# Causal attention with its transfers further ahead: load 8 (was 6), relative product 6 (was 5), skewed read 4 (was 3), and SyncE issuing load, read, write

## The chip, the cores and the metric

The kernel runs on one core of a Trainium2 chip. The metric is device time in microseconds for one execution of the whole program: a two-layer block of attention and feed-forward parts. The change lies in one of its stages, the causal attention of the first layer.

## The reference

```python
# layer 0 attention; q from layernorm(x), k and v from ctx; B=4, S=512, 16 heads of 16, so 64 heads
QEr = jnp.einsum('bhsd,ld->bhsl', q, Er_s)
Srel = _skew(QEr)                          # row i is shifted so that column j holds q_i . Er[511 - (i - j)]
QK = jnp.einsum('bhsd,bhtd->bhst', q, k)
attn = (QK + Srel) / math.sqrt(dh)
attn = jnp.where(causal[None, None], attn, -jnp.inf)
attn = jax.nn.softmax(attn, axis=-1)
out = jnp.einsum('bhst,bhtd->bhsd', attn, v)
# then x = x + out, a top-2-of-8 expert feed-forward, a masked attention and a ternary-weight feed-forward
```

## The kernel before

**The stage.** `causal_attention` takes 64 heads (4 batches of 16), one a step, as a software pipeline. A head is 512 queries by 512 keys, of which only the causal part is made: `CAUSAL_UNITS` packs the row blocks 512, 384+128 and 256 columns wide into three units, 1280 columns (REL_W) on 128 partitions. Queries and keys are held as bf16 pieces in DRAM (`packed`), 96 partitions a head.

**One head's way through the stages:**
1. *Load* (SyncE, line 424, by `load_head`, line 309): the head's queries and keys from DRAM into `qk`, 192 KB; 8 buffers (ROUND).
2. *Relative product* (TensorE `relative`, line 442; ScalarE copy, line 552): Q times Er into `psE`, copied into `stage`, 2 buffers.
3. *Write* (SyncE, line 429): `stage` into the DRAM tensor `rel`, 640 KB; 4 slots (RING).
4. *Skewed read* (SyncE, line 419): `rel` back into `bias`, each partition starting one column earlier, which is the reference's `_skew`; 640 KB; 4 buffers.
5. *Scores* (TensorE, lines 450 and 453, into `psS`) and on VectorE, line 512, scores plus bias with the row maximum.
6. *Exponential* (ScalarE, line 557), one step later.
7. *Transposes* (TensorE, line 464, `psT`; VectorE copy, line 520), another step later, and the weighing of the values by groups of four heads (lines 353, 366, 373, 375).

**What sets the order.** Each engine runs its own `step(n)`, n from -LOAD on. In step n an engine works on head n + k for each stage, k being that stage's lead: LOAD, REL, READ, SOFT (the scores), EXP. `stage_of` gives head, slot and turn. The first and last steps are unrolled, the middle ones loop eight at a time (`run_heads`). Engines keep pace by semaphores alone. On SyncE, which issues all three transfers of a head through one queue and waits in program order, these are:
- the read waits until the head's write has landed, and until VectorE is done with the bias buffer that it overwrites (4 heads back);
- the load waits until TensorE has made the scores of the head 8 back;
- the write waits for ScalarE's three copies, and for the read 4 heads back.

ScalarE waits in front of a head's copies until the write two heads back has landed (line 545), because `stage` has two buffers; its exponentials of the same step stand behind that wait. In the last steps SyncE also fills `slots_in` with zeros for the next stage (line 432).

Of the kernel before, what the change touches and what calls it, by code (L numbers as in the profile page):

```python
# [33 lines left out]
ROUND = 2 * GROUP  # L34
# [10 lines left out]
def wait(eng, sem, value):  # L45

    if isinstance(value, int) and value <= 0:
        return
    eng.wait_ge(sem, value)  # L49


def build(nc, a, out):
# [14 lines left out]
    with top:  # L67
        def sem(name):
            return nc.alloc_semaphore(name)

        def sb(ctx, name, shape, dt=F32):
            return ctx.enter_context(nc.sbuf_tensor(name, shape, dt))
# [211 lines left out]
        def run_heads(eng, first, last, step):  # L284

            for n in range(first, ROUND):
                step(n, n % ROUND, n // ROUND)
            rounds = NBH // ROUND - 2
            with eng.Fori(1, rounds + 1) as it:
                for r in range(ROUND):  # L290
                    step(it * ROUND + r, r, it)
            for n in range((rounds + 1) * ROUND, last + 1):
                step(n, n % ROUND, n // ROUND)

        def stage_of(n, r, it, ahead):

            if isinstance(n, int) and not 0 <= n + ahead < NBH:
                return None
            return n + ahead, (r + ahead) % RING, it * (ROUND // RING) + (r + ahead) // RING
# [8 lines left out]
        def load_head(sp, m, dst, s_qk):  # L308
            sp.dma_start(dst, bass.AP(packed.ap().tensor, m * (DH * 2 * S),
                                      [[B * D * 2 * S, PIECES], [2 * S, DH], [1, 2 * S]])).then_inc(s_qk, 16)  # L310
# [69 lines left out]
        def causal_attention(ErP, identb, dmask):  # L380

            units = CAUSAL_UNITS
            NU = len(units)
# [1 line left out]
            place = {i: (512 * u + off, w) for u, unit in enumerate(units) for i, off, w in unit}  # L385
            key_place = {j: (512 * u + off, w) for u, unit in enumerate(CAUSAL_KEYS) for j, off, w in unit}
            last = NBH + 2 * GROUP
            LOAD, REL, READ, SOFT, EXP = 6, 5, 3, 2, 1
            with ExitStack() as ctx:
                qk = [sb(ctx, f"qk{r}", [KP, 2 * S], BF16) for r in range(ROUND)]  # L390
                stage = [sb(ctx, f"stage{r}", [P, REL_W]) for r in range(2)]
# [9 lines left out]
                s_qk = [sem(f"s_qk{r}") for r in range(ROUND)]  # L401
# [3 lines left out]
                s_emm, s_eev, s_smm, s_soft, s_nm, s_exp, s_tmm, s_tev, s_seen, s_seen_sp = (  # L405
                    sem(f"s_{n}") for n in names)
                block = ctx.enter_context(nc.Block())

                @block.sync
                def _(sp):  # L410
                    def step(n, r, it):
                        if h := stage_of(n, r, it, READ):
                            m, slot, turn = h
                            sp.wait_ge(s_wr[slot], 16 * (turn + 1))
                            sp.sem_inc(s_seen_sp, 1)
                            wait(sp, s_soft, NU * (m - RING + 1))

                            skewed = bass.AP(rel[slot].ap().tensor, P - 1, [[REL_W - 1, P], [1, REL_W]])
                            sp.dma_start(bias[slot][:, :], skewed).then_inc(s_rd[slot], 16)
                        if h := stage_of(n, r, it, LOAD):  # L420
                            m, slot, turn = h
                            wait(sp, s_smm, NU * (m - ROUND + 1))
                            slot = (r + LOAD) % ROUND
                            load_head(sp, m, qk[slot][:, :], s_qk[slot])
                        if h := stage_of(n, r, it, REL):
                            m, slot, turn = h
                            sp.wait_ge(s_eev, NU * (m + 1))
                            wait(sp, s_rd[slot], 16 * turn)
                            sp.dma_start(rel[slot][:, :], stage[slot % 2][:, :]).then_inc(s_wr[slot], 16)
                        if isinstance(n, int) and n + READ == NBH:  # L430

                            sp.dma_start(slots_in[:, :].rearrange("(n p) d -> p n d", p=P),
                                         zero_row[:, :].unsqueeze(1).broadcast_to([P, SLOT_TILES, D])).then_inc(s_zeroed, 16)
                    run_heads(sp, -LOAD, last, step)
# [284 lines left out]
        with ExitStack() as ctx:  # L719
# [108 lines left out]
            with ExitStack() as c0:  # L828
                ErP = sb(c0, "ErP", [KP, S], BF16)
                with nc.cleanup_on_exit():  # L830
                    opening(ErP)
                    causal_attention(ErP, identb, dmask)
# [861 lines left out]
```

## Time and profile before

| what | us |
|---|---|
| median of 3 runs (1341.21 to 1344.07) | 1343.36 |
| the profiled execution, from first to last instruction (its only time on record) | 1343.2 |
| the causal attention stage, by its first load and the next stage's first transfer | 81.07 to 455.07 |
| writes of heads 8 to 63 issued, the steady part | 128.76 to 431.01 |

Over the span PE is busy 1048.0 us (78%), VectorE 696.9 (52%), ScalarE 655.3 (49%). The page cuts the span into 40 slices of 33.6 us; the stage is the third to the fourteenth. Each digit is a share in tenths, and GB/s is what the DMA engines moved:

```profile
PEclk9866978798889777799999999566899999998799
DMA  7477877787778866666656652235311111110001
GB/s 246 163 254 273 287 269 277 255 283 272 264 267 291 320 261 217 218 192 199 211 186 205 206 190 95 79 105 190 100 47 47 47 47 47 44 44 9 0 25 40
```

### The profile page before, as it was taken

The numbers are of one execution on the slowest core, as the hardware profiler recorded it, in microseconds if no ns is written. First come the engines' busy times: TensorE is split into PE (matmuls) and PEld (weight loads), VectorE is DVE, ScalarE is ACT, GpSimd is POOL, SyncE is SP. The second block draws the span as 40 slices with busy tenths as digits, with TensorE's granted clock in tenths as the row PEclk, the third lists the DMA queues.
The fourth block names the chain that finished last, engine by engine and source line by source line (L and its number), as shares of the span: only waits on it lengthen the run. The fifth ranks groups of instructions, "written<-read, shape, count | busy, mean of one in ns | idle before, by whom it ended". The sixth has DMA issues, their size and how long they took to land. (4 is left out here: it accounts for less than half of the span.)

```text
span 1343.2 us, 22770 instructions
## 1 busy us (share of the span) xinstructions
PE 1048.0 (78%) x6434; PEld 648.0 (48%) x6435; DVE 696.9 (52%) x2140; ACT 655.3 (49%) x1346; POOL 224.2 (17%) x531
## 2 busy tenths in 40 slices
PE   6736787777778384699999999133899999997487
PEld 3414444444444252599999998011233333333444
DVE  4825666676667763110111100346766666674687
ACT  2425666666566221233333232132677777763687
POOL 0000000000000026011111111530222222231222
PEclk9866978798889777799999999566899999998799
DMA  7477877787778866666656652235311111110001
GB/s 246 163 254 273 287 269 277 255 283 272 264 267 291 320 261 217 218 192 199 211 186 205 206 190 95 79 105 190 100 47 47 47 47 47 44 44 9 0 25 40
DMA packets 93319, 227.41 MB, mean 169 GB/s; under 512 B 9686, under 2 KB 51766, under 8 KB 87254
## 3 DMA queue, kind: packets, MB, share of 16 engines
q1 hardware_dynamic: 86454, 208.20, 45.1%
q0 software_dynamic: 6816, 18.62, 5.0%
q8 instruction: 22, 0.36, 0.1%
q14 instruction: 27, 0.22, 0.0%
HBM read 143.07 MB, written 83.62 MB: 169 GB/s over the span
## 5 line engine op out<-in xcount | busy, mean ns | idle before, releaser
L684 DVE CUSTOM_DVE_ANT_0 unused<-mpsS,mask_bias 128x512 bf16<-128x512 f32 x256 | 172.1, 691 | 84.0 <-PE mpsS L617 83.8
L711 ACT ACTIVATE mPT<-mpsB 128x512 f32<-128x512 f32 x256 | 152.8, 598 | 81.0 <-PE mpsB L624 74.8
L1358 ACT ACTIVATE hT<-ph,w 128x128 f32<-128x128 f32 x312 | 89.3, 369 | 197.0 <-PE ph L1332 197.0
L512 DVE CUSTOM_DVE_ANT_0 scores<-psS,bias 128x512 f32<-128x512 f32 (+3 forms) x256 | 120.1, 488 | 113.2 <-PE psS L453 57.5
L552 ACT COPY stage<-psE 128x512 f32<-128x512 f32 (+1 forms) x192 | 98.2, 513 | 148.8 <-PE psE L442 144.9
L464 PE MATMUL psT<-ident,scores 128*128 128x128 f32 x640 | 120.9, 310 | 44.5 <-ACT scores L557 42.6
L1332 PE MATMUL ph<-xT,w 128*128 128x128 f32 x1248 | 147.0, 276 | 0.0
L1377 DVE TENSOR_TENSOR ys<-py,b 128x256 f32<-128x256 f32 x39 | 16.6, 425 | 249.3 <-PE py L1342 249.3
L1332 PEld LDWEIGHTS ph<-xT,w 128*128 128x128 f32 x1248 | 143.9, 193 | 0.1
L1342 PE MATMUL py<-w,hT 128*128 x624 | 141.2, 379 | 0.7 <-DVE ys L1377 0.7
L557 ACT ACTIVATE scores<-scores,nm 128x128 f32<-128x128 f32 (+3 forms) x256 | 136.4, 562 | 4.4 <-DVE nm L525 4.4
L442 PE MATMUL psE<-ErP,qk 96*128 96x512 bf16 (+3 forms) x256 | 79.7, 358 | 59.4 <-DMA qk<-packed 58.4
L1342 PEld LDWEIGHTS py<-w,hT 128*128 128x128 f32 x624 | 115.6, 190 | 15.2 <-issue 1.1
L520 DVE COPY PT<-psT 128x512 f32<-128x512 f32 (+1 forms) x192 | 114.7, 599 | 10.7 <-PE psT L464 10.5
L617 PE MATMUL mpsS<-mqk 96*128 96x512 bf16 x256 | 100.7, 395 | 21.2 <-DMA mqk<-packed 15.5
L464 PEld LDWEIGHTS psT<-ident,scores 128*128 128x128 f32 x640 | 77.5, 159 | 69.0 <-ACT scores L557 50.7
L622 PE MATMUL mpsB<-mqk 99*128 99x512 bf16 x256 | 98.8, 386 | 0.1
L624 PE MATMUL mpsB<-maskT,identb 128*128 128x512 bf16 x256 | 98.1, 383 | 0.0
L339 POOL TENSOR_TENSOR spreada<-V,zerosa 128x272 f32<-128x272 f32 x16 | 11.5, 721 | 423.2 <-PE psOa L353 341.5
L450 PE MATMUL psS<-qk 96*128 96x512 bf16 (+3 forms) x256 | 80.8, 341 | 1.0 <-DVE mx L512 0.8
L353 PE MATMUL psOm<-mPT,spreadm 128*32 128x512 f32 x512 | 67.8, 604 | 0.8 <-ACT headsm L360 0.8
L617 PEld LDWEIGHTS mpsS<-mqk 96*128 96x128 bf16 x256 | 25.0, 98 | 87.0 <-DVE mmx L684 36.3
(247 smaller groups left out, 1501.0 us busy)
## 6 DMA issues: line engine op xcount, KB each, us to landing
rel<-stage SPq DMA_DIRECT2D x64, 640.0 KB, 3.8
bias<-rel SPq DMA_DIRECT2D x64, 640.0 KB, 5.6
w<-in_w1p SPq DMA_DIRECT2D x39, 1028.0 KB
qk<-packed SPq DMA_DIRECT2D x64, 192.0 KB
mqk<-packed SPq DMA_DIRECT2D x64, 192.0 KB
w<-in_w2p SPq DMA_DIRECT2D x8, 1024.0 KB
slots_in<-zero_row SPq DMA_DIRECT2D x1, 4992.0 KB, 18.2
xs<-slots_in SPq DMA_DIRECT2D x39, 128.0 KB
```

The costliest lines, as they stand in the source:

```text
L464: tr = nc.tensor.transpose(psT[bank][:, to:to + P], scores[slot][:, at:at + P], ident[:, :])
L512: ttr = nc.vector.tensor_tensor_reduce(out=scores[slot][:, at:at + w], in0=psS[(NU * slot + u) % 2][:, off:off + w], in1=bias[slot][:, at: ...
L520: nc.vector.tensor_copy(PT[r][:, 512 * u:512 * u + WU[u]], psT[(NU * slot + u) % 2][:, 0:WU[u]]).then_inc(s_tev, 1)
L552: nc.scalar.copy(stage[slot % 2][:, 512 * i:512 * i + WU[i]], psE[(NU * slot + i) % 2][:, 0:WU[i]]).then_inc(s_eev, 1)
L557: ex = nc.scalar.activation(scores[slot][:, at:at + w], scores[slot][:, at:at + w], ACT.Exp, bias=nm[:, slot, i:i + 1], scale=1.0 / 4)
L617: nc.tensor.matmul(psS[i % 2][:, :], qk[slot][0:KP, i * P:(i + 1) * P], qk[slot][0:KP, S:2 * S], start=True, stop=True).then_inc(s_smm, 1)
L622: nc.tensor.matmul(psB[i % 2][:, :], qk[slot][:, S + i * P:S + (i + 1) * P], qk[slot][:, 0:S], start=True, stop=False)
L624: nc.tensor.matmul(psB[i % 2][:, :], identb[:, :], maskT[:, i, :], start=False, stop=True).then_inc(s_bmm, 1)
L684: nc.vector.tensor_tensor_reduce(out=unused[:, i, :], in0=psS[i % 2][:, :], in1=mask_bias[:, i, :], scale=1.0, scalar=-3.0e38, op0=ALU.add ...
L711: nc.scalar.activation(PT[r][:, j, :], psB[j % 2][:, :], ACT.Exp, scale=1.0 / 4).then_inc(s_exp, 1)
L1332: mm = nc.tensor.matmul(ph[half][:, q * P:(q + 1) * P], w1[i][:, dk * F + f * P:dk * F + (f + 1) * P], xT[i][:, dk, :], start=(dk == 0), s ...
L1342: mm = nc.tensor.matmul(py[:, 0:D], hT[i][:, f, :], w2[:, bass.ds(e, 1), f * D:(f + 1) * D].rearrange("p a d -> p (a d)"), start=(f == 0), ...
```

## The change

The leads change, so that the load of a head goes out in step m-8 (was m-6), its relative product and write in step m-6 (was m-5), its read in step m-4 (was m-3). Scores, exponentials and transposes keep their steps. SyncE issues load, read, write in each step, where it issued read, load, write. The pipeline starts at step -8. No buffer, size or other instruction changes.

```diff
-            LOAD, REL, READ, SOFT, EXP = 6, 5, 3, 2, 1
+            LOAD, REL, READ, SOFT, EXP = 8, 6, 4, 2, 1
@@
                     def step(n, r, it):
+                        if h := stage_of(n, r, it, LOAD):
+                            m, slot, turn = h
+                            wait(sp, s_smm, NU * (m - ROUND + 1))
+                            slot = (r + LOAD) % ROUND
+                            load_head(sp, m, qk[slot][:, :], s_qk[slot])
                         if h := stage_of(n, r, it, READ):
                             m, slot, turn = h
                             sp.wait_ge(s_wr[slot], 16 * (turn + 1))
@@
                             sp.dma_start(bias[slot][:, :], skewed).then_inc(s_rd[slot], 16)
-                        if h := stage_of(n, r, it, LOAD):
-                            m, slot, turn = h
-                            wait(sp, s_smm, NU * (m - ROUND + 1))
-                            slot = (r + LOAD) % ROUND
-                            load_head(sp, m, qk[slot][:, :], s_qk[slot])
                         if h := stage_of(n, r, it, REL):
```

## Rows read from the trace of the kernel before

**Rows 1.** Window of the steady part: bounds, length, busy by engine, PEclk, DMA share, GB/s

```profile
125.00:431.00 306.00, 234.41 (x1724) 136.87 (x1724) 205.42 (x697) 189.14 (x404) 9.38 (x13) 0.89 0.78 275
```

**Rows 2.** Waits, 125 to 431 us: engine, tile, line, what for, total, times, longest

```profile
ACT stage L552 <- PE psE L442: 113.0, 74, 4.6
PE psE L442 <- DMA qk<-packed: 35.8, 37, 3.2
DVE scores L512 <- DMA bias<-rel: 28.0, 26, 3.3
```

**Rows 3.** Timeline of SyncE's queue (start, length); writes of heads 8, 31 to 34, 63

```profile
128.76 0.33 SPq L429 DMA_DIRECT2D rel<-stage  x1
...
248.54 0.32 SPq L419 DMA_DIRECT2D bias<-rel  x1
249.07 0.85 SPq L309 DMA_DIRECT2D qk<-packed  x1
252.43 0.33 SPq L429 DMA_DIRECT2D rel<-stage  x1
...
261.38 0.33 SPq L429 DMA_DIRECT2D rel<-stage  x1
...
267.39 0.33 SPq L429 DMA_DIRECT2D rel<-stage  x1
...
271.74 0.33 SPq L429 DMA_DIRECT2D rel<-stage  x1
...
431.01 0.32 SPq L429 DMA_DIRECT2D rel<-stage  x1
```

**Rows 4.** Timelines of PE and DVE; in brackets idle time before and its releaser

```profile
202.12 0.39 PE L442 MATMUL psE<-ErP,qk 96*128 96x512 bf16 x1 [0.90 <-DMA qk<-packed]
...
256.05 0.69 DVE L512 CUSTOM_DVE_ANT_0 scores<-psS,bias 128x512 f32<-128x512 f32 x1 [3.26 <-DMA bias<-rel]
...
257.46 0.61 PE L442 MATMUL psE<-ErP,qk 96*128 96x512 bf16 x1 [3.22 <-DMA qk<-packed]
```

**Rows 5.** From issue to landing, 125 to 431 us: the write's line, then the read's

```profile
DMA to landing us min/median/max: 3.1/3.8/6.1
...
DMA to landing us min/median/max: 4.4/5.9/7.7
```

**Rows 6.** Windows of 2 us, columns as in rows 1

```profile
125.00:127.00 2.00, 1.61 (x13) 1.19 (x14) 1.38 (x4) 0.45 (x1) 0.00 (x0) 1.00 1.14 303
...
203.00:205.00 2.00, 2.00 (x12) 1.57 (x11) 1.49 (x6) 1.01 (x4) 0.00 (x0) 0.50 0.61 231
...
255.00:257.00 2.00, 0.00 (x0) 0.00 (x0) 0.95 (x3) 0.00 (x0) 0.00 (x0) 1.00 1.00 351
...
259.00:261.00 2.00, 2.00 (x14) 1.30 (x16) 1.79 (x8) 0.98 (x3) 0.00 (x0) 0.50 0.08 26
...
427.00:429.00 2.00, 1.34 (x11) 0.92 (x12) 1.38 (x4) 0.19 (x1) 0.00 (x0) 1.00 1.03 342
```

**Rows 7.** DMA issues of the page: count, KB each, median us to landing

```profile
rel<-stage SPq DMA_DIRECT2D x64, 640.0 KB, 3.8
bias<-rel SPq DMA_DIRECT2D x64, 640.0 KB, 5.6
...
qk<-packed SPq DMA_DIRECT2D x64, 192.0 KB
```

**Rows 8.** Timelines of PE and DVE at the stage's start and end

```profile
93.55 1.04 PE L442 MATMUL psE<-ErP,qk 96*128 96x512 bf16 x3 [4.31 <-DMA qk<-packed]
...
436.68 0.69 DVE L512 CUSTOM_DVE_ANT_0 scores<-psS,bias 128x512 f32<-128x512 f32 x1 [0.88 <-issue]
...
440.15 0.69 DVE L512 CUSTOM_DVE_ANT_0 scores<-psS,bias 128x512 f32<-128x512 f32 x1
```

**Rows 9.** The step 267.39 to 271.74: ScalarE's first copy, and the step's window

```profile
269.45 0.59 ACT L552 COPY stage<-psE 128x512 f32<-128x512 f32 x1 [0.96 <-PE psE L442]
...
267.39:271.74 4.35, 4.31 (x39) 2.18 (x32) 3.04 (x11) 3.27 (x8) 0.00 (x0) 1.00 0.86 291
```

## The prediction

> **What bounds the kernel now.** I took the stage's place from the page's slices, then read its window, the waits, the issue times of SyncE's queue, and last the two-microsecond windows. The change touches one stage, the causal attention, which lies at 80 to 455 us. In its steady part, 125 to 431 us, no engine is full: PE is busy 234 of 306 us, DVE 205, ACT 189, the DMA share is 0.78 and the granted clock averages 0.89 [rows 1]. So the stage is not limited by one resource's capacity, and what it waits for decides.
>
> The waits name two transfers. PE waits 35.8 us for `qk` (the head's load) in front of the relative product, DVE 28.0 us for `bias` (the skewed read) in front of the first score reduction. ACT's larger wait, 113.0 us for psE, is what they look like one engine further on [rows 2].
>
> One stall in detail shows how. Head 31's write goes out at 252.43 and head 32's only at 261.38, 8.95 us later [rows 3]. Between them DVE stands 3.26 us until head 29's read lands at 256.05, and PE, behind DVE's bank release and its own load, 3.22 us until head 32's load lands at 257.46 [rows 4]. That read was issued at 248.54 and that load at 249.07 [rows 3], so they took 7.5 and 8.4 us; in the steady part a read takes 4.4 to 7.7 us from issue to landing, median 5.9, a write 3.1 to 6.1, median 3.8 [rows 5]. By the code a read is issued one step ahead of its use (READ 3, SOFT 2) and so is a load (LOAD 6, REL 5). One step is 4.35 us when nothing is late (267.39 to 271.74) [rows 3]. A transfer of 5.9 us ordered one 4.35 us step ahead is late; that is the bound: latency under load, at too short a distance.
>
> The stall is paid twice. During it PE is idle (0.00 busy in 255 to 257) and the granted clock then falls from 1.00 to 0.50, 1.2 GHz [rows 6]. At that clock the next step, 261.38 to 267.39, takes 6.01 us although it waits for no transfer [rows 3]. And with the engines late nothing new is ordered: the DMA share falls to 0.08 at 259 to 261 [rows 6], after having been at 1.00. The DMA engines are thus alternately full and empty.
>
> **The pace now.** Head 8's write is issued at 128.76 and head 63's at 431.01: 55 intervals in 302.25 us, 5.50 us a head [rows 3].
>
> **What the change does, part by part.**
>
> *Load 8 ahead, product 6 ahead.* A load now has two steps instead of one before its product. Two steps of 4.35 us are 8.7 us, above even the 8.4 us of the bad case. The buffer: head n+8 takes the slot of head n, whose scores PE makes in step n-2, since SOFT is 2. SP enters step n after ACT's copies of step n-1, so this wait (it had four steps of slack, now two) ends before it is reached. Gain: PE's 35.8 us of waits. New wait: none.
>
> *Read 4 ahead.* A read also has two steps instead of one, 8.7 us against at most 7.7. Its own condition, the write of the same head, stays two steps earlier (6-4 as 5-3), and the bias buffer it overwrites, head n's, was used by DVE in step n-2. Gain: DVE's 28.0 us. It overlaps PE's waits: in the stall above, 3.26 and 3.22 us together cover only 4.7 us, 0.72 of their sum [rows 4], so I count the two as 0.72 x 64 = 46 us.
>
> *Order load, read, write.* The read may stand behind a write that hasn't landed (longest 6.1 us) [rows 5], and then no longer holds up the load. Each issue still costs SP 0.33 us for a write, as much for a read and about 0.8 for a load [rows 3]: about 1.5 us of a step, and SP idles for most of the rest. The read now goes out some 0.9 us later, behind the load's issue. That is covered by the whole step that it gained. If that cover were gone it would be 0.9 us a step, 50 us over the stage; it would need reads over 7.8 us.
>
> *The clock.* A mean of 0.89 between levels 1.00 and 0.50 is 22% of the 306 us, 67 us, at half clock. Steps there take 6.01 instead of 4.35 us: 67 x (1 - 4.35/6.01) = 18 us lost. Without long stalls most of it returns.
>
> *What is late next.* Taking all of both away gives 302 - 46 - 18 = 238 us, 4.33 us a head: the fast step again. But the DMA engines must move 640 + 640 + 192 KB a head, 1.507 MB [rows 7]. Of the 153 windows of 2 us from 125 to 431 us, 54 have a DMA share of 0.95 or more and move on average 326 GB/s; the first, the last and one in the stall stand in [rows 6]. So a full DMA side needs 1.507 / 0.326 = 4.62 us a head. From the mean (275 GB/s at share 0.78) it would be 1.507 / 0.353 = 4.27 us [rows 1]. The slower figure is the nearer one, being measured when full. DMA therefore becomes the bound, with the engines at 4.35 close behind; two near-equal bounds with jitter give somewhat more than either. Bounds for the new pace: 4.35 us (fast step) from below; from above 5.50, no gain. I take 4.8, close to the full-DMA row, plus 0.2 for jitter and an occasional low-clock step.
>
> *Steady part:* 55 x (5.50 - 4.8) = 38 us less.
>
> *Ends.* The pipeline gets one step more between product and scores. At the start head 0 still has to go load, product, write, read, score; what changes is that head 2's load no longer waits for the first write (PE idles 4.31 us for it until 93.55 [rows 8]), so head 8's write comes one step earlier relative to the scores, 5 to 6 us. At the end there is one step more after the last write; steps there have no product and take 3.5 us (436.68 to 440.15 [rows 8]). Net about 2 us less, bounds 0 and 5. The zero fill of slots_in still follows the last read and has the tail's time to itself as now.
>
> Sum: 38 + 2 = 40 us off the profiled span of 1343.2 us, which stands 0.2 us from the median of 1343.36: 1303 us.
>
> **A rule against the rows.** The windows show 326 GB/s with all 16 DMA engines occupied, writes, skewed reads and loads mixed [rows 6]. The Trainium skill (DMA: Bandwidth & Descriptors, section Anatomy of one DMA) gives a variable cost of bytes over 436 GB/s. By it a head needs 3.46 us and DMA would bound nothing. The rows at full share move a quarter less, so the trace disagrees and the sum goes by them.
>
> **Rivals.**
>
> *A. The engines bound, DMA keeps up.* Pace 4.45 (4.35 to 4.5, the shortest steps): 55 x 1.05 + 2 = 60 us less, 1283. For: the mean-share figure of 4.27 us, and transfers that are spread evenly may run better than in bursts. Against: 54 full windows at 326 GB/s. The skill's rate above would lead here.
>
> *B. The clock keeps falling.* At a DMA-bound pace PE still pauses in every step. If it spends the same 22% of time at half clock, the rate is 0.22/6.01 + 0.78/4.8, a pace of 5.02: 55 x 0.48 + 2 = 28 us less, 1315; with 40% low, 5.22: 17 us less, 1326. For: not every fall follows a long stall; 203 to 205 reads 0.50 and the wait ahead of it was 0.90 us [rows 4, 6]. Against: at 267 to 272 PE is busy 4.31 of 4.35 us and keeps 1.00 [rows 9]. The Trainium skill (TensorE: Matmul & The Clock Gate, section A second HAM failure mode: psum-queue depth-cycling) tells of a kernel whose short pauses between groups alone made the clock oscillate; this stage does rotate through two banks per product.
>
> *C. The transfers only get slower.* More of them in flight lengthen each other, as 7.5 and 8.4 us in the stall showed, and the waits return at two steps' distance: pace 5.4 to 5.5, 1337 to 1343. Against: the share of 0.78 and the empty windows.
>
> *D. The write's landing takes over, slower.* ACT may copy head n+6 only when head n+4's write has landed (two stage buffers), and it waits in front of its exponentials, so PE's transposes and DVE's copies stand behind. The loop: first copy to the write's issue takes 2.29 us (269.45 to 271.74 [rows 3, 9]), then the landing L, and two heads pass per turn: pace (L + 2.29)/2. With L 3.8 it is 3.0, with 6.1 4.2: hidden. It decides from L = 2 x 4.8 - 2.29 = 7.3 us, and is slower than before from L = 8.7. Loads and reads ordered earlier stand in front of the write, so L may grow; at 9.2 us the pace is 5.75, 14 us more, 1357. Against: a write would have to take 2.6 us longer than the longest now, and the loop throttles itself before.
>
> *E. The change doesn't do what it says*, for instance a read or load held back by the buffer conditions above. Then pace and time stay; held to be part of C.
>
> **Numbers.** Forecast (pace 4.6 to 5.0) 0.54; A 0.12; B 0.23; C with E 0.06; D 0.05. A measurement of this kernel can tell a change of 0.2%, 2.7 us, from none. Faster: forecast, A, B and a part of C, 0.91. Same: most of C, 0.05. Slower: 0.04. The range reaches from near A, pace 4.5 (1343 - 57 = 1286), to B's bad end with a little over, 1330, leaving out about 0.2.
>
> **What would show it.** PE's waits for qk and DVE's for bias in the stage near zero after the first heads; the pace of SP's write issues near 4.8 with no interval of 7 us; DMA share over 0.9 and 310 GB/s or more; granted clock over 0.95; reads landing later than now (6 us or more) without anyone waiting. Wrong would be: a share of 0.8 with a clock of 1.00 (then the engines bound, A), a clock still at 0.9 or below (B), ACT waiting for the rel DMA at the copy of line 552 (D).

## The result and the profile after

The changed kernel takes 1283.9 us (median of 4 runs, 1282.46 to 1286.1) against 1343.58 us (now of 4 runs): ratio 0.9563, 95% interval 0.9543 to 0.9583. It is faster by 60 us where I had forecast 40, and lies 2 us below the low end of my range. The profiled execution has a span of 1284.6 us.

The slices of the page, now of 32.1 us each; the stage is the third to the thirteenth:

```profile
PEclk9865999999996877999999997576999999998799
DMA  7478889999998657665666641345211111110001
GB/s 247 149 258 307 321 329 337 344 341 339 337 324 329 237 180 240 189 214 185 208 196 195 208 147 50 103 157 155 63 47 46 47 44 48 44 38 9 1 29 39
```

From the fifth slice to the twelfth the clock digit is 9 throughout, where it went up and down, and the DMA engines move 321 to 344 GB/s, where the kernel before moved 255 to 291.

The steady part, between the writes of heads 8 and 63, answers to [rows 1, 3]; these are SyncE's timeline (start, length), and the window between, with its busy times, clock, DMA share and GB/s:

```profile
125.86 0.33 SPq L429 DMA_DIRECT2D rel<-stage  x1
...
371.10 0.32 SPq L429 DMA_DIRECT2D rel<-stage  x1
...
397.23 0.38 SPq L1074 DMA_DIRECT2D mask<-in_mask  x1
```

```profile
125.86:371.10 245.24, 194.69 (x1690) 120.09 (x1691) 201.45 (x684) 180.00 (x399) 9.35 (x13) 1.00 0.91 335
```

55 intervals in 245.24 us are 4.46 us a head, against 5.50. The longest is 5.31 us, where it was 8.95. VectorE's work is the same as before (202 us) in 57 us less. Head 8's write comes 2.9 us earlier, the part from the last write to the next stage's first transfer is 2.1 us longer (26.1 against 24.1, the additional step), and the rest of the program 0.8 us shorter: 57.0 + 2.9 - 2.1 + 0.8 = 58.6 us, the difference of the spans.

The waits of the changed kernel over 200 to 360 us, a part of what [rows 2] cover:

```profile
ACT stage L552 <- DMA rel<-stage: 41.6, 36, 1.3
...
PE psT L464 <- ACT scores L557: 31.4, 36, 1.4
DVE scores L512 <- DMA bias<-rel: 13.6, 23, 0.7
```

PE's wait for `qk` is gone. DVE still waits for `bias`, here never over 0.7 us. What is new stands on top: ScalarE waits in every step of this stretch, 1.16 us on average, for its write two heads back to land (over the whole steady part 60.4 us in 51 waits, the longest 1.7, and DVE 24.2 us in 34, the longest 1.3). PE's transposes wait for ScalarE's exponentials behind it. This is the loop of rival D. It can be read in one step (SyncE's timeline, then ScalarE's):

```profile
246.88 0.32 SPq L429 DMA_DIRECT2D rel<-stage  x1
247.42 0.78 SPq L309 DMA_DIRECT2D qk<-packed  x1
...
253.67 0.33 SPq L424 DMA_DIRECT2D bias<-rel  x1
255.75 0.32 SPq L429 DMA_DIRECT2D rel<-stage  x1
```

```profile
253.69 0.58 ACT L552 COPY stage<-psE 128x512 f32<-128x512 f32 x1 [1.28 <-DMA rel<-stage]
```

The write issued at 246.88 has landed at about 253.65. At that moment both who waited for it go on: SyncE's read of that head and ScalarE's first copy. 2.1 us later the copies are done and the write two heads on goes out, at 255.75. Two heads in 8.87 us are 4.43 a head. The landings of writes over the steady part, then of reads, against [rows 5]:

```profile
DMA to landing us min/median/max: 3.6/6.7/7.5
...
DMA to landing us min/median/max: 5.7/7.2/8.3
```

Writes take 6.7 us instead of 3.8. (6.7 + 2.1)/2 = 4.4, near the pace of 4.46. This says where the wait is. Whether the loop is also the limit, e6 tells further down.

### The profile page after: what moved, and what is told of

It reads as the page before. It is cut to its first block and busy times, and to the rows that moved or that the text cites. A ratio compares the mean times of both kernels' runs of the same rounds, so it can differ in the third digit from the quotient of the medians.

```text
span 1284.6 us, 22764 instructions
## 1 busy us (share of the span) xinstructions
PE 1011.8 (79%) x6434; PEld 632.7 (49%) x6435; DVE 696.2 (54%) x2140; ACT 647.5 (50%) x1346; POOL 223.0 (17%) x531
## 5 line engine op out<-in xcount | busy, mean ns | idle before, releaser
L464 PE MATMUL psT<-ident,scores 128*128 128x128 f32 x640 | 108.6, 286 | 58.0 <-ACT scores L557 56.1
L552 ACT COPY stage<-psE 128x512 f32<-128x512 f32 (+1 forms) x192 | 97.5, 510 | 97.6 <-DMA rel<-stage 70.8
L464 PEld LDWEIGHTS psT<-ident,scores 128*128 128x128 f32 x640 | 69.3, 145 | 81.7 <-ACT scores L557 59.6
L442 PE MATMUL psE<-ErP,qk 96*128 96x512 bf16 (+3 forms) x256 | 71.1, 323 | 20.8 <-DMA qk<-packed 16.1
L450 PE MATMUL psS<-qk 96*128 96x512 bf16 (+3 forms) x256 | 73.8, 314 | 1.8 <-DVE mx L512 1.8
```

What stands on the lines that cost most here:

```text
L464: tr = nc.tensor.transpose(psT[bank][:, to:to + P], scores[slot][:, at:at + P], ident[:, :])
L552: nc.scalar.copy(stage[slot % 2][:, 512 * i:512 * i + WU[i]], psE[(NU * slot + i) % 2][:, 0:WU[i]]).then_inc(s_eev, 1)
```

## The experiments

The runs come in six sets: the result, e1 to e4, e5 to e8, e9 to e12, e13 to e16, e17 and e18. The part of the program behind the stage, which only the experiments with another row layout touch, took 887 to 892 us in some sets (the result, e9 to e12, e17 and e18) and 865 to 870 in the others, with medians of the kernel before of 1343 to 1347 and of 1318 to 1322. What makes these 22 us is open; the record has the same chip number for e1 to e4 and for e17 and e18, which fall on either side. So ratios are to the kernel before in the same set, and the stage is compared by the *pace* (write of head 8 to write of head 63, over 55) and the *stage's end* (the next stage's first transfer; the stage's first load goes out at 80.5 to 83.0 in all of them). Both come from one profiled execution each, which in e3, e5 and e13 was the fastest of its kernel in that set and in the changed kernel's first, e4 and e16 the slowest, so small differences of them weigh little.

| kernel | ratio (95%) or us | pace | stage's end |
|---|---|---|---|
| before | 1343.6 | 5.50 | 455.1 |
| e9 before, again | 1340.3, one run | 5.34 | 446.5 |
| e2 order alone | 1.0004 (0.9972 to 1.0036) | 5.42 | 450.6 |
| e4 read lead alone | 1.0036 (1.0014 to 1.0057) | 5.58 | 462.6 |
| e3 load lead alone | 0.9772 (0.9736 to 0.9807) | 4.85 | 415.1 |
| e1 all leads, old order | 0.9682 (0.9643 to 0.9721) | 4.71 | 410.7 |
| changed | 0.9563 (0.9543 to 0.9583) | 4.46 | 397.2 |
| e5, e16 changed, again | 0.9581 (0.953 to 0.9632), 0.9560 (0.9524 to 0.9595) | 4.45, 4.44 | 394.2, 396.6 |
| e17 7, 5, 3, new order | 1.0018 (0.999 to 1.0047) | 5.44 | 454.3 |
| e10 8, 5, 3, new order | 1.0034 (1.0005 to 1.0063) | 5.50 | 458.4 |
| e6 changed, 4 stage buffers | 0.9604 (0.9555 to 0.9653) | 4.51 | 397.3 |
| e7 half of the read left out | 1258.2, one run | 4.38 | 389.0 |
| e8 the same, 4 stage buffers | 1251.7, one run | 4.36 | 384.2 |
| e11, e18 light engines, 4 stage buffers | 1297.9, 1293.5, one run each | 4.72, 4.69 | 406.4, 403.9 |
| e14 light engines, 2 stage buffers | 1261.7, one run | 4.48 | 391.5 |
| e12 changed, each head loaded twice | 1397.9, one run | 6.36 | 507.4 |
| e13 changed, contiguous rows | 0.9497 (0.946 to 0.9534) | 4.36 | 384.4 |
| e15 before, contiguous rows | 0.9725 (0.9671 to 0.978) | 4.83 | 416.0 |

### Which part did it: e1 to e4, e9

```diff
e1: LOAD, REL, READ = 8, 6, 4   SyncE: read, load, write (as before)
e2: LOAD, REL, READ = 6, 5, 3   SyncE: load, read, write (as changed)
e3: LOAD, REL, READ = 7, 5, 3   SyncE: read, load, write
e4: LOAD, REL, READ = 7, 6, 4   SyncE: read, load, write
```

e1: 

> The new leads 8, 6, 4 with SyncE's old order read, load, write. Theory 1 (the leads do it: each transfer has two steps to land in): within 3 us of the changed kernel's 1284, pace of the writes 4.46 us. Theory 2 (the order does a good part, since a read that waits for its write held up the load): half of the gain or less, 1300 to 1315, pace about 4.8.

e2: 

> The old leads 6, 5, 3 with the new order load, read, write. Theory 1: the load goes out 0.9 us earlier and the read as much later, a gain on one wait and a loss on the other; 1335 to 1348, clock still about 0.89. Theory 2 (the order does a good part): 1310 or less.

e3: 

> Leads 7, 5, 3 in the old order: only the load gets a second step. Theory 1: PE's waits for qk (35.8 us in the steady part) go, DVE's for bias (28.0) stay, and with them falls of the clock; two late transfers share one stall, so less than half of the gain of 60 us: 1320 (1312 to 1332). Theory 3 (the load alone was the cause and the read's waits were its echo): 1290 or less and DVE's waits for bias under 5 us.

e4: 

> Leads 7, 6, 4 in the old order: only the read gets a second step, the load stays one step ahead of its product. Theory 1: DVE's waits for bias go, PE's for qk stay at 30 us or more: 1325 (1315 to 1335). Theory 4 (the read alone was the cause): 1290 or less and PE's waits for qk under 5 us.

e9: 

> The kernel before itself, for its trace on a chip of this group. The part of the program behind the stage (from the next stage's first transfer to the end) took 888 us in the two shown profiles and 865 to 867 in the later ones; if the chip alone makes that difference it is 866 here too, while the stage ends at about 452 (450 to 456) with a pace near 5.4.

The order alone gives nothing, as expected, but not by standing still: PE's waits for qk nearly go (2.5 us, from 35.4), DVE's for bias grow to 70.8 (from 26.8), and the clock is 0.95. The load's second step alone gives about half of the gain (2.3% of 4.4%), more than I had put down: DVE's waits for bias stay, as expected (they even grow, to 42.6 us), but the clock is at 0.96 and the pace at 4.85. The read's second step alone gives nothing, even a little loss: DVE's waits for bias go, PE's for qk stay (40.2 us), so does the clock, 0.88. Theory 1 had both transfers late in one stall; these runs show that a read on time helps only when the load is too, and that a load on time helps by itself in the old order (e3) and not in the new one (e2). e1 falls between its theories: 13.5 to 16.5 us of the stage belong to the order once the leads are there. e9 misses its expectation: its part behind the stage took 892 us, and its stage still ended at 446.5. So the stage of the kernel before ended 9 us apart in two executions, that of the changed kernel 3 us apart in three. The 13 runs of the kernel before in e9's set spread over 13.6 us by themselves, so this needs no change of chip. That it varies because it stands on the edge of its transfers is a reading of mine, not shown.

### What the order does: e17, e10

e17 is e3 in the new order, e10 gives the load a third step.

e17: 

> Leads 7, 5, 3 with the order load, read, write. If the order undid e10 (the load's bytes go in front of a read that is needed one step later): about the time of the kernel before, ratio 0.99 to 1.01, DVE's waits for bias 60 us or more. If the third step did: ratio about 0.977 as in e3, DVE's waits about 43 us.

e10: 

> Leads 8, 5, 3 with the order load, read, write: the load has three steps, the read one. Theory 3 (the load alone was the cause; the read's second step is worth little): stage ends at 397 to 401, pace 4.45 to 4.55. Theory 1 (a read of 6 to 7 us ordered one step ahead is late by itself): DVE's waits for bias stay at 40 us or more, pace 4.8 to 4.9, stage ends at 413 to 419.

Both gain nothing. The order undid e3, not the third step. With a read ordered one step ahead, the load's bytes in front of it make it late: DVE's waits for bias are 64.2 and 77.4 us, against e3's 42.6. e10 misses both of its theories, which had paces of 4.9 at most. With the read two steps ahead the same order gains 1% (e1 against e5, whose sets are of the same kind). The reason can be read from SyncE's timeline in e1, where the read waits in the queue for its write to land and holds up the load until just before the next write:

```profile
249.83 0.33 SPq L429 DMA_DIRECT2D rel<-stage  x1
252.23 0.33 SPq L419 DMA_DIRECT2D bias<-rel  x1
252.82 0.77 SPq L309 DMA_DIRECT2D qk<-packed  x1
254.31 0.33 SPq L429 DMA_DIRECT2D rel<-stage  x1
```

There writes land after 7.1 us, and ScalarE's copies need 2.1: (7.1 + 2.1)/2 = 4.6, the median of e1's intervals; its pace, the mean, is 4.71. In the changed kernel the load goes out right behind the previous write, 0.54 us after it, and only the read stands in front of the next: 6.7 us, 4.46. That the load's place makes these 0.4 us is argued from the two timelines.

### Engines or transfers: e5 to e8

```diff
e6 (and e8)
-   stage = [sb(ctx, f"stage{r}", [P, REL_W]) for r in range(2)]
+   stage = [sb(ctx, f"stage{r}", [P, REL_W]) for r in range(RING)]     # and stage[slot], waits for head m - 4
e7, e8
-   skewed = bass.AP(rel[slot].ap().tensor, P - 1, [[REL_W - 1, P], [1, REL_W]])
+   skewed = bass.AP(rel[slot].ap().tensor, P - 1, [[REL_W - 1, P], [1, REL_W // 2]])   # the rest of bias is zero
```

e5: 

> The changed kernel itself, beside the others on this chip. If the order load, read, write is worth something with the new leads, its stage ends earlier than that of the leads alone (next stage's first transfer 410.7 us there): expected 397 and a pace of 4.46. If the difference between the two profiles was the chip's, it ends at 410.

e6: 

> The changed kernel with four stage buffers, so that ScalarE waits for the write four heads back. Theory L (the loop write, landing, copies sets the pace: (6.7 + 2.2)/2 = 4.45): ScalarE's 70 us of waits for the rel DMA go and the pace falls to that of the engines, 4.35 or less, 6 us or more less in all. Theory Q (the DMA queue is full at this pace, and the landing time is only how full it is): ScalarE's waits go too, but DVE's for bias grow in their place, the landings get longer than 7 us and the pace stays at 4.42 to 4.46. Theory E (VectorE and ScalarE set it): pace stays and nothing grows.

e7: 

> The changed kernel reading only the first 640 of 1280 bias columns back (the rest of the bias is zero: part of the computation is left out), so a head moves 1.18 MB instead of 1.507. Theories L and Q: landings fall to about 5 us, ScalarE's waits for rel go, and the pace falls to what the engines can do. Theory E: pace stays at 4.46. If the pace falls to 4.35 the engines were 0.1 us behind the transfers, if below 4.2 the transfers cost more than I put down.

e8: 

> The same with four stage buffers: no transfer waits at all are expected, so this pace is that of the engines by themselves. Theory L and Q: the same pace as with two buffers, within 0.03 us. DVE's busy time gives a floor of about 4.1 us.

e5 repeats the changed kernel in another set: the order's part is real. With half of the read left out (e7, e8) the pace is 4.38 and 4.36, no interval over 4.9, ScalarE's waits for rel gone, writes landing in 4.5 and 4.3 us. That is what the engines can do; 4.34 is the interval they repeat. (VectorE is busy 3.7 us of a head in e8, not the 4.1 of its expectation, so it alone is no floor.) The changed kernel stands 0.1 us above it. Four stage buffers (e6) take ScalarE's waits away, and half of the intervals are 4.36 us or less, but some grow (longest 5.87) and the mean is 4.51: the landing grows to 7.7 us in exchange. Of the theories Q comes nearest, though it had the pace at 4.46 at most: the wait was where the transfers' limit showed, not the limit.

### What limits the transfers: e11, e12, e14, e18

e11 (again as e18) and e14 leave nearly all of VectorE's and ScalarE's work out, with four and two stage buffers; e12 loads each head twice.

```diff
e11, e14, e18: every width w of exponential, score reduction and PT copy becomes 32
e12
    load_head(sp, m, qk[slot][:, :], s_qk[slot])
+   wait(sp, s_x[h[1]], 16 * turn)
+   load_head(sp, m, extra[h[1]][:, :], s_x[h[1]])
```

e11: 

> The changed kernel with four stage buffers, in which the exponentials, the score reductions and the copies of the transposed probabilities work on the first 32 columns only (most of the attention is left out), so VectorE and ScalarE are nearly idle and all transfers stay. Its pace is what the DMA queue can do, or TensorE's 3.6 us. My forecast's figure (326 GB/s when full) says 4.62; the stage with four buffers already ran 4.51, so 4.3 to 4.5 if the DMA engines are the bound behind it, and under 4.1 if that stage's bumps were not the queue's.

e12: 

> The changed kernel loading each head twice, the second time into a buffer that nobody reads: 1.704 MB a head. If the transfers are close to their capacity at 338 GB/s, the pace rises to 1.704 / (0.338 to 0.350) = 4.87 to 5.04. If they had room (by the mean share 0.91, 0.4 us a head), it stays under 4.7.

e14: 

> The light engines of e11 (exponentials, reductions and copies on 32 columns only, most of the attention left out) with two stage buffers as in the changed kernel. If a deeper queue is slower, the pace is below e11's 4.72, near 4.4 to 4.5; if the queue's own rate is 4.72 whatever its depth, it is 4.7 or more.

e18: 

> e11's kernel once more (most of the attention left out, four stage buffers). If a queue that is kept full delivers less, the pace is 4.65 to 4.75 again on whatever chip, against e14's 4.48. If the chip made the difference, a chip whose rest of the program takes 866 to 869 us shows 4.5 or less.

e11 missed its expectation: with idle engines the pace is *slower* than in the changed kernel, 4.72 (e18: 4.69), at a DMA share of 0.97 and 318 GB/s, while e14, with two buffers, has 4.48 at 0.91 and 337. The windows of e11, then of e14:

```profile
120.43:379.86 259.43, 207.10 (x1690) 116.45 (x1691) 72.94 (x684) 139.11 (x400) 9.41 (x13) 0.99 0.97 318
```

```profile
120.53:367.14 246.61, 201.73 (x1689) 122.53 (x1690) 75.36 (x684) 126.68 (x399) 9.34 (x13) 0.99 0.91 337
```

The higher share moves less. So the queue kept full by four buffers delivers less than the one held back by two. This is not fully settled: e11 and e18 have 890 and 888 us behind the stage, e14 has 869, and e18, run to separate depth from set, again came into a set of the slower kind. For it: the changed kernel had the same pace in both kinds of sets (4.46 and 4.45), and e6 against e5, in one set, goes the same way (4.51 against 4.45).

e12 was the surprise. 13% more bytes make the pace 6.36 us, 43% slower, at a share of only 0.78; writes land after 10.7 us and (10.7 + 2.1)/2 = 6.4. It misses both of its theories (5.04 at most). The DMA share in slices of 0.5 us, 240 to 260 us, tells why:

```profile
DMA  3439779999974335979999997333396999999734
GB/s 154 158 147 240 205 309 387 307 338 340 391 311 191 147 158 180 238 252 309 297 283 309 420 383 291 154 158 137 158 246 250 367 276 244 315 391 391 301 154 164
```

For 1.5 to 2 us of each of e12's steps the share is 0.3 to 0.4, at about 155 GB/s. In the changed kernel it falls that low only for single slices. A share that sits there is 6 of 16 engines, 0.375. The stage's start, before its first write, shows the same with loads alone in the queue; first the changed kernel, then e13 below, whose load has another layout:

```profile
84.00:85.00 1.00, 0.00 (x0) 0.00 (x0) 0.00 (x0) 0.00 (x0) 0.03 (x1) 0.50 0.36 127
```

```profile
83.00:84.00 1.00, 0.23 (x1) 0.13 (x2) 0.00 (x0) 0.00 (x0) 0.71 (x1) 0.50 0.89 219
```

The load's DRAM pattern has the outermost dimension PIECES = 6. The Trainium skill (DMA: Bandwidth & Descriptors, section Why a DMA increments its semaphore by 16 and not by 1) states the rule: a transfer runs on the largest number of engines up to 16 that divides the slowest dimension of both sides, so 6 here and 16 for the 128-partition writes and reads. The trace agrees. The packets under 512 bytes, which are of 4 bytes in its records, number 2067 in the changed kernel's 55 steps, 38 a head as 16 + 16 + 6 would have it; in e12 they are 44, one load of 6 more, and in e13 2608, 47 of 48. The two views, of the changed kernel and of e13:

```profile
DMA packets 21154, 82.16 MB, mean 335 GB/s; under 512 B 2067, under 2 KB 2067, under 8 KB 21146
```

```profile
DMA packets 21846, 82.92 MB, mean 346 GB/s; under 512 B 2608, under 2 KB 2608, under 8 KB 21839
```

Six engines then carry a sixteenth of write and read each, 80 KB, and a sixth of the load, 32 KB: 112 KB where an even split has 92. An estimate from e12's stretches: if six engines together move 155 GB/s, their 672 KB of a head take 4.44 us. That is the pace of the changed kernel (4.44 to 4.46) and of e14 with nearly idle engines (4.48), so these six are the likely bound, and the loop's wait only shows it. The same estimate gives 5.7 us for e12, which took 6.36, and it cannot say why e1 takes 4.71 and e11 4.72 with the same bytes. That part stays open.

### The cause tried: e13, e15, e16

```diff
-   packed = dram("packed", (PIECES, B, D, 2, S), BF16)
+   packed = dram("packed", (B, D, PIECES, 2, S), BF16)
-   rows = packed[:, b, eh * P:(eh + 1) * P, self.side, :].rearrange("g e s -> e g s")
+   rows = packed[b, eh * P:(eh + 1) * P, :, self.side, :]
-   m * (DH * 2 * S), [[B * D * 2 * S, PIECES], [2 * S, DH], [1, 2 * S]]
+   m * (KP * 2 * S), [[2 * S, KP], [1, 2 * S]]
-   bass.AP(er_t, 0, [[0, PIECES], [S, DH], [1, S]])
+   bass.AP(er_t, 0, [[S, DH], [0, PIECES], [1, S]])
-   rows = slice(g * DH, (g + 1) * DH)
+   rows = slice(g, KP, PIECES)
```

The products contract over the 96 rows, so their order is free as long as both sides share it.

e13: 

> The changed kernel with the 96 rows of a head contiguous in DRAM (and the rows of qk and ErP in that order), so that a load's outermost dimension is 96 and not 6; bytes and all else as they are. Theory S (a load runs on 6 of 16 engines and these six set the pace of the queue): the stretches at share 0.3 to 0.4 go, the landing of a write falls from 6.7 to about 5 us, ScalarE's 60 us of waits for rel go, the pace is the engines' 4.36, 5 us or more less in all. Theory Q (the sum of the bytes is the limit): nothing changes but the share's pattern, pace 4.44 to 4.46.

e15: 

> The kernel before (leads 6, 5, 3, order read, load, write) with contiguous rows for a load. Theory S: the load lands sooner, PE's waits for qk (31 to 35 us) fall to a third or less, and the stage gains 20 us or more without any change of the leads: pace 5.0 or less. Theory Q: within 5 us of the kernel before.

e16: 

> The changed kernel on this chip, as the baseline of e13: pace 4.45 to 4.47, stage ends at 394 to 397.

Theory S holds. e13's window, waits and landings of writes:

```profile
118.36:358.25 239.89, 194.04 (x1689) 119.90 (x1690) 200.85 (x685) 185.74 (x399) 9.36 (x13) 1.00 0.98 346
```

```profile
ACT stage L551 <- PE psE L441: 48.3, 55, 1.1
PE psT L463 <- ACT scores L556: 46.3, 55, 1.7
```

```profile
DMA to landing us min/median/max: 3.7/4.5/6.4
```

The same bytes, at 346 GB/s, land in 4.5 us; no transfer is in the list of waits any more, and the pace is 4.362, that of e8, the engines' own. The first heads gain more than the steady part, by the profiles: from the first load to head 8's write 37.4 us against 43.8 in e16, where 55 steps of 0.08 us make 4.5. In the same set e13 takes 1251.9 us (1248.61 to 1255.09) and the changed kernel 1262.4 (1259.99 to 1267.75): it beats both kernels, 5.0% faster than before. e15 shows the other side: with a load on all engines, the old leads alone give 4.83 instead of 5.3 to 5.5. PE's waits for qk fall to 15.6 us, about half, not to a third as expected, and DVE's for bias stay (43.9). So the load's layout was a good part of what made it late at one step's distance. Two things change along with the number of engines and were not separated from it: a head's rows lie in one piece of DRAM instead of six, and SyncE's issue of a load takes 0.3 to 0.5 us instead of 0.8.

## Why the prediction was wrong

**Right: what bound the kernel before.** Transfers ordered one step ahead of 4.35 us, landing in 4 to 8, and the clock's fall behind each stall. After the change the waits for qk are gone, the clock is 1.00 in the steady part, and the share no longer falls to nothing. The fast step of 4.35 is the engines' pace, as e7, e8 and e13 show. The clock's 18 us were not measured by themselves; e2, with a clock of 0.95 and no gain, warns that a mean clock alone isn't time. Rival B did not come: PE still stands before its transposes in every step (50.6 us in 55 waits, the longest 1.7), and the clock stays at 1.00, so short pauses did not lower it here. Of C only the first half came: landings grow (writes from 3.8 to 6.7 us, reads from 5.9 to 7.2), but two steps cover them.

**Right: the ends,** 2 us forecast, 0.8 measured. Here two errors cancel: the start gains 2.9 us and not 5 to 6, the end costs 2.1 and not 3.5.

**The step that failed** is the one called what is late next: "a full DMA side needs 1.507 / 0.326 = 4.62 us", and 0.2 on top for jitter, hence 4.8. Measured: 4.46, so 0.34 x 55 = 19 us of the miss. It failed in two ways. The rate of the windows at a share of 0.95 or more is no capacity. In the changed kernel 47 of 120 such windows move 386 GB/s on average, where 54 of 153 moved 326; e11 shows 318 at 0.97 and e13 346 at 0.98. The share is the time of packets, and packets last longer in a fuller queue: by the trace's records one of 5120 bytes takes 0.25 us on average in e11 and 0.22 in e14. The sum also took the 16 engines as one, where the load uses six of them. And jitter cost next to nothing: 48 of the 55 intervals are 4.33 to 4.6 us, the longest 5.31.

**Rival A** had the number (1283, pace 4.45) but not the reason. The engines do 4.36; the 0.1 us above it belongs to the transfers (e13 takes it away).

**Rival D** had the wait, with the loop (L + 2.29)/2. I dismissed it below L = 7.3, having compared it with a pace of 4.8 that wasn't there. With the copies at 2.1 us (1.8 in e14) the loop gives the measured pace, within about 0.1 us, in the changed kernel (L = 6.7), in e1 (7.1), e14 (7.0) and e12 (10.7). But L follows from how full the transfers are, and e6, which takes the loop away, gains nothing. So the loop tells the pace without being its cause. Its bad end would have been slower, and e12 shows how near that is: one more load of 192 KB brings the program to 1398 us.

**The order** I had at nothing, "0.9 us later, covered by the whole step". That holds with the new leads and it even gains there; with a read one step ahead it costs 2.5% (e17's ratio against e3's).

**The 436 GB/s** of the Trainium skill (DMA: Bandwidth & Descriptors, Anatomy of one DMA) would have led to rival A's time. That section gives it for transfers that GpSimd issues; here SyncE does. No steady part here moved more than 346 GB/s on average, so the rate remains unshown.

## What to carry to other kernels

When a transfer is late at a distance of one step, give it a second one before making it smaller, and look first at the one that lands last: here the load's step was worth 2.3%, the read's nothing without it. Then compute each ring's loop (landing plus work, over buffers) with the landing that the fuller queue will have, because the next wait shows there, and test by one more buffer whether the loop is the limit or only shows it. And a DMA share that rests at a fraction such as 6/16 points to a transfer cut on few engines; its outermost dimension is the thing to change.

## What the runs showed of the hardware

- Loads of 96 rows laid out as 6 x 16, alone in the queue, hold the DMA share at 0.36 (127 GB/s); laid out as 96 contiguous rows they reach 0.89 (219 GB/s). Among other transfers the first layout leaves stretches at a share of 0.3 to 0.4 and about 155 GB/s (e12). A second such load cost 1.9 us a head, where 192 KB at the stage's 337 GB/s are 0.6.
- The DMA share isn't a measure of room: 268 GB/s at 0.78 (e12, at its limit) and 274 at 0.78 (the kernel before, with room for 22% more).
- The same program took 887 to 892 us behind the stage in some sets of runs and 865 to 870 in others; within one set the kernel before spread over 13.6 us.
